# A decoder layer on one core: two heads' value products in one column group, maxima split before they are turned, routing within the cross half

## The chip, the core and the metric

The kernel runs on one core of a Trainium2 chip. The core has a tensor engine (PE, with its weight loads as PEld), VectorE (DVE), ScalarE (ACT), GpSimd (POOL) and SyncE (SP), each with its own queue of instructions; they wait for one another by semaphores. Matmul results stand in PSUM, in 8 banks of 128 partitions x 512 fp32 columns. The metric is the device time of one launch in microseconds.

## The reference

64 sequences of 128 tokens, width 128, 16 heads of 8; a context of 77 tokens per sequence. One decoder layer:

```python
x = x + attn(layernorm(x))                    # q,k,v = h Wq', h Wk', h Wv'; softmax(q k' / sqrt(128)) v, then Wff' + bff
x = x + xattn(layernorm(x), ctx, ctx, mask)   # with bq, bk, bv; softmax(masked q k' / sqrt(8)) v, then Wo' + bo
h = layernorm(x)                              # experts
gate = l2norm(h Wp') . l2norm(sim) / temperature          # 8 experts
top_v, top_i = top_k(gate, 2);  p = softmax(top_v)
x = x + sum over the two of p_e * (gelu(h W1[e] + b1[e]) W2[e] + b2[e])
```

The bias bv of the cross values goes through a softmax whose weights sum to 1, and then through Wo: it adds the constant bv Wo' to every token.

## The kernel before

Stage A holds the attentions, the norms and the routing. It works on blocks of 4 sequences (NS = 4, 16 blocks), in a software pipeline of steps t = -3 to 19, all written out. A step has two halves. In the self half (X, `in_x`) PE makes the exponent scores of self attention of block t and, in between, the scores from which the maxima of block t+1 come; in the cross half (Y, `in_y`) the exponent scores of cross attention of block t-2 and the maxima scores of block t-1. A half has 16 units of 4 heads (half of one sequence's heads of one group g), and 3 more to run out. In each unit u PE does 4 score products for the maxima (`scores`, L982), 4 for the exponent (`shifted`, L998), in every second unit the value products of two units (`values`, L1018), and then what `in_x(u)` or `in_y(u)` hangs on: turnings (transposes), projections, the ranks. Each engine's code has the same steps and the same u, and thus its own fixed order.

Value products: the weight of a head is 32 columns wide (`VW`): 8 values, a column of ones for the denominator, zeros. 4 heads of a unit go to the 4 column groups of PE side by side (partitions 32c to 32c+31 of a bank), and the four units of a sequence fill one bank `pv`. ACT copies each bank to `oT` (L594), PE turns it in four pieces (`outputs_T`, L1048, units 0 to 3 of the next half), DVE divides by the denominator (`divide`, L741, L743). Then the result is turned back (u = 5) and projected (u = 7), DVE adds the residual (u = 8) and takes the norm's statistics.

Maxima: DVE takes them from the score bank (L731). PE turns the negated maxima (`maxima_T`, L961, u = 6), and they are split into three bf16 shares in the turned shape of 16 x 512: ACT (L559), DVE (L719), ACT (L566), POOL (L440). SP writes them to DRAM and reads them back under the stacked queries (`fold`), where they shift the exponent.

Two working banks, `wb[0]` and `wb[1]`, serve all that hangs on: `claim` makes PE wait until the last user of a bank has been read (`drained`).

Norms: DVE statistics, `lnve` (L705), POOL the power -1/2 (L431), DVE `lnnm` (L710), ACT the normalising in four pieces (L572).

Routing of block t-3: the gate's product in Y at u = 10, 11; `choose` on DVE in Y at u = 16 (gate values, the top two, marks, running sums `before`); in X of the next step `weigh` (u = 10), the ranks on PE (u = 15, three products, L1093 to L1097) and `route` (u = 16), which gives each token its two slots. POOL scatters the rows to the experts' lists (`enlist`, 8 indirect DMAs per block, L457), paced by PE's units.

Stage B (`phase_b`) runs over 39 tiles of 512 listed rows and the two expert products; it is not changed. Between the stages DVE builds a table of tiles, and the pipeline has drained.

## Time and profile before

| | us |
|---|---|
| median of 3 runs | 1223.12 |
| lowest, highest | 1222.99, 1224.07 |
| the profiled execution | 1220.65 |
| its span | 1218.9 |
| PE busy in the span | 1027.5 (84%) |
| DVE, ACT, POOL busy | 874.9, 842.9, 552.5 |

The span is what the profile shows between the first and the last instruction. A busy PE is not a PE at its peak, since matmuls are pipelined and their ends are modelled: what a group costs the queue is the distance from its start to the start of the next one, and not its own duration. An engine's idle time before an instruction stands in brackets, with what ended it.

### The profile page before, as it was taken

To read this page: it belongs to the slowest core of one execution; us is meant where nothing else is said; L and a number is where in the kernel's file an instruction comes from. 1 tells how busy PE (TensorE), PEld (TensorE's weight loads), DVE (VectorE), ACT (ScalarE), POOL (GpSimd) and SP (SyncE) were. 2 spreads that over 40 slices of the span, in tenths; PEclk is the share of its full clock that TensorE was granted. 3 is DMA by queue.
4 is the path that set the end of the run, shared out by engine and by line. 5 is a ranking of instruction groups with operands and counts; after the bars stand their busy time and mean duration, and the time that the engine had idled before them with its cause. 6 is when DMAs were issued, how large, how long until landed. Compare 5 with 4: busy or idle time off the path is not lost. (4 is left out here: it accounts for less than half of the span.)

```text
span 1218.9 us, 32475 instructions
## 1 busy us (share of the span) xinstructions
PE 1027.5 (84%) x11795; PEld 792.2 (65%) x11795; DVE 874.9 (72%) x2569; ACT 842.9 (69%) x1729; POOL 552.5 (45%) x550
## 2 busy tenths in 40 slices
PE   2467789999999999999999999967709999999940
PEld 1255567777777777777767777745507888888730
DVE  2655657778788787787887786654367888888846
ACT  1255567778777877777787777644509999998940
POOL 4312323245545544554555444433442666665650
PEclk9877899999999999999999999988858999999985
DMA  4327574473474454545544631430252444232219
GB/s 93 94 74 162 140 162 99 118 180 91 124 173 106 125 150 117 135 130 122 150 110 115 169 92 39 103 78 28 94 191 74 113 118 125 84 79 77 79 43 374
DMA packets 120334, 144.24 MB, mean 118 GB/s; under 512 B 34056, under 2 KB 98472, under 8 KB 115376
## 3 DMA queue, kind: packets, MB, share of 16 engines
q1 hardware_dynamic: 108832, 120.37, 38.8%
q0 software_dynamic: 9168, 17.21, 4.5%
q10 hardware_dynamic: 2176, 4.59, 1.1%
q8 instruction: 95, 1.56, 0.6%
q14 instruction: 63, 0.52, 0.1%
HBM read 88.42 MB, written 55.36 MB: 118 GB/s over the span
## 5 line engine op out<-in xcount | busy, mean ns | idle before, releaser
L584 ACT ACTIVATE probs<-sc_a 77x512 f32<-77x512 f32 (+1 forms) x512 | 300.6, 590 | 122.7 <-PE sc_a L998 51.8
L1295 POOL DMA_INDIRECT y_d<-yo,row x156 | 159.9, 1025 | 117.0 <-issue 81.4
L731 DVE TENSOR_REDUCE negm_m<-sc_m 128x4 f32<-128x512 f32 x256 | 174.1, 684 | 42.9 <-PE sc_m L982 41.1
L731 DVE TENSOR_REDUCE negm_cm<-sc_m 128x4 f32<-128x308 f32 x256 | 119.8, 474 | 108.2 <-PE sc_m L987 102.6
L457 POOL DMA_INDIRECT xs_d<-xrow,slot_i x128 | 127.8, 999 | 141.9 <-PE sc_a L1003 103.9
L1018 PE MATMUL pv<-probs,big 128*32 128x128 f32 x4096 | 165.5, 281 | 0.3
L1390 DVE TENSOR_TENSOR gl<-g,gh 128x512 fp32r<-128x512 f32 x156 | 107.5, 690 | 35.5 <-ACT g L1339 26.7
L1018 PEld LDWEIGHTS pv<-probs,big 128*32 128x32 f32 x4096 | 97.2, 110 | 54.6 <-issue 36.6
L982 PE MATMUL sc_m<-ks,qs 96*128 96x128 bf16 x1024 | 104.6, 229 | 32.2 <-DMA ks<-stk_k 14.0
L982 PEld LDWEIGHTS sc_m<-ks,qs 96*128 96x128 bf16 x1024 | 72.7, 101 | 78.6 <-issue 51.1
L998 PE MATMUL sc_a<-cqs,cks 102*77 102x128 bf16 x1024 | 100.9, 221 | 6.5 <-DMA cqs<-cmscr 6.0
L998 PE MATMUL sc_a<-qs,ks 102*128 102x128 bf16 x1024 | 101.8, 223 | 1.8 <-ACT probs L584 1.8
L1003 PE MATMUL sc_a<-identb,mbias 128*77 128x512 bf16 x256 | 99.2, 387 | 0.0
L998 PEld LDWEIGHTS sc_a<-cqs,cks 102*77 102x77 bf16 x1024 | 89.1, 118 | 14.3 <-issue 6.7
L982 PE MATMUL sc_m<-cks,cqs 96*128 96x77 bf16 x1024 | 79.9, 201 | 20.1 <-DMA cqs<-cmscr 12.7
L982 PEld LDWEIGHTS sc_m<-cks,cqs 96*128 96x128 bf16 x1024 | 63.8, 99 | 41.5 <-issue 23.7
L1048 PE MATMUL wb<-ident,oT 128*128 128x128 f32 x512 | 79.0, 279 | 7.6 <-DVE rest_q L721 5.1
L987 PE MATMUL sc_m<-mbias,identb 128*128 128x308 bf16 x256 | 78.0, 305 | 0.0
L594 ACT ACTIVATE oT<-pv 128x512 f32<-128x512 f32 x128 | 75.9, 593 | 2.4 <-PE pv L1018 1.5
L440 POOL TENSOR_TENSOR parts_m<-rest_k,parts_m 16x512 bf16<-16x512 f32 x32 | 36.7, 1148 | 80.1 <-ACT parts_m L566 80.1
L998 PEld LDWEIGHTS sc_a<-qs,ks 102*128 102x128 bf16 x1024 | 70.1, 99 | 3.9 <-ACT probs L584 2.7
L435 POOL TENSOR_TENSOR xres<-xagain,bff_b 128x512 f32<-128x512 f32 x16 | 20.4, 1274 | 115.2 <-DMA xagain<-x_dram 115.2
(201 smaller groups left out, 2546.7 us busy)
## 6 DMA issues: line engine op xcount, KB each, us to landing
xg<-xs_d SPq DMA_DIRECT2D x39, 260.0 KB
stk_q<-parts_q SPq DMA_DIRECT2D x16, 384.0 KB, 2.5
stk_k<-parts_k SPq DMA_DIRECT2D x16, 384.0 KB
qs<-stk_q SPq DMA_DIRECT2D x16, 384.0 KB
ks<-stk_k SPq DMA_DIRECT2D x32, 192.0 KB
stk_cq<-parts_cq SPq DMA_DIRECT2D x16, 384.0 KB, 2.9
cqs<-stk_cq SPq DMA_DIRECT2D x16, 384.0 KB, 5.4
xin<-x_dram SPq DMA_DIRECT2D x16, 256.0 KB
```

The lines of the kernel that those rows point to most:

```text
L457: nc.gpsimd.indirect_dma_start(out=xs_d, in_=row[:, c // 2, c % 2, :], in_offset=None, out_offset=bass.IndirectOffsetOnAxis(ap=slot_i[:, c ...
L584: nc.scalar.activation(probs[e % 4][0:rows], sc_a[e % 2][0:rows], ACT.Exp, scale=scale)\
L594: nc.scalar.activation(oT[n][:, s, :], pv[s % 2][:], ACT.Copy).then_inc(oT_ok[n].sem, 1)
L731: nc.vector.tensor_reduce(out=negm[n][:, s, g, 4 * half:4 * half + 4], in_=sc_m[u % 2][:, 0:4 * cols].rearrange("p (j k) -> p j k", j=4), ...
L982: i = nc.tensor.matmul(sc_m[u % 2][:, j * cols:(j + 1) * cols], qst[0:KR, 4 * half + j, s * S:(s + 1) * S], kst[0:KR, HG * g + 4 * half + ...
L987: i = nc.tensor.matmul(sc_m[u % 2][:, 0:4 * cols], identb[:], bias[:, s, :].unsqueeze(1).broadcast_to([128, 4, cols]), start=False, stop=T ...
L998: i = nc.tensor.matmul(sc_a[u % 2][0:cols, j * S:(j + 1) * S], kst[:, HG * g + 4 * half + j, s * cols:(s + 1) * cols], qst[:, 4 * half + j ...
L1003: i = nc.tensor.matmul(sc_a[u % 2][0:cols, :], bias[:, s, :], identb[:].unsqueeze(1).broadcast_to([128, 4, S]), start=False, stop=True, sk ...
L1018: i = nc.tensor.matmul(pv[s % 2][32 * c:32 * c + VW, (u % 4) * S:(u % 4 + 1) * S], va[:, s, HG * g + 4 * half + c, :], probs[u % 4][:, c * ...
L1048: i = nc.tensor.transpose(wb[s % 2][:, slot * S:(slot + 1) * S], oT[n][:, s, slot * S:(slot + 1) * S], ident[:])
L1295: nc.gpsimd.indirect_dma_start(out=y12_d, in_=yo[par][:, c, :], in_offset=None, bounds_check=2 * B * S - 1, oob_is_err=False, out_offset=b ...
L1390: nc.vector.tensor_tensor(out=gl[c][:], in0=g[c][:], in1=hi32(gh[c][:]), op=ALU.subtract).then_inc(gl_ok.sem, 1)
```

## The change

1. Two heads, one of each group g, share a column group: their weights are 32 wide as before, but the first has its 8 values and its one in the columns 0 to 8, the second in 16 to 24 (`in_pair`). The second product adds to what the first left (start only at g = 0). Two sequences fill one bank. `oT` has 2 pieces per block (`NO`), so there are 2 copies, 2 groups of turnings and 2 divisions (of 32 x 8 values) per block and half, at u = 0 and 1. The steps behind them move up: turning back at u = 3, projection at 5, residual at 6, statistics at 7. The columns of Wv and the rows of Wff and Wo are put in the new order on the host as they were in the old.
2. Maxima: POOL splits them before they are turned (`shares`, four operations on 64 columns). PE then turns the three shares in one go as four bf16 products with the shares as weights, and one ACT copy of 48 x 512 takes them out.
3. Norms: `lnve` and `lnnm` are POOL's; DVE keeps the statistics.
4. Routing of block t-3 stands in the cross half: gate product at u = 8, 9, `choose` at 12, `mark` at 13, ranks at 15, `weigh` at 15, `route` at 16, with fewer and wider operations; running sums are made by more rank products (3 + 1 to 4 + 4) and not by DVE. The row numbers come from an iota on POOL. The scatters are spread over the whole next step, with two sets of slots.
5. The cross value bias: bv Wo' is added to the output bias once at the start (one product, one addition); ACT copies the cross values where DVE added the bias.
6. The self value product moves from u = 4 to 12 of the cross half, and the turned x2 to bank 1 at u = 14, with cross Q at 16.

The core of the diff (declarations, and the like edits of the second attention, left out):

```diff
-        negm = {n: sa(f"negm_{n}", [128, NS, 2, HG]) for n in ("m", "cm")}
+        negm = {n: sa(f"negm_{n}", [128, NS, H]) for n in ("m", "cm")}
+        left = sa("left", [128, NS, H])
+        third_m = sa("third_m", [128, NS, 3, H], BF16)
...
-        oT = dict.fromkeys("sc", sa("oT", [128, NS, T]))
+        oT = dict.fromkeys("sc", sa("oT", [128, NO, T]))
...
+        def in_pair(tile):
+
+            return tile.rearrange("p q g w -> p q (g w)").rearrange("p q (a b) -> p q a b", b=OW)[:, :, 0:4:3, :]
...
-                    pool.wait_ge(ln_ve[n].sem, ln_ve[n].val(b))
+
+                    pool.wait_ge(ln_st[n].sem, ln_st[n].val(b))
+                    wait_block(pool, ln_ok[n], b - 1)
+                    nc.gpsimd.tensor_scalar(lnve[n][:], lnmv[n][:, :, 1], LN_EPS, None, ALU.add).then_inc(ln_rs[n].sem, 1)
+                    nc.gpsimd.tensor_scalar(lnnm[n][:], lnmv[n][:, :, 0], -1.0, None, ALU.mult).then_inc(ln_rs[n].sem, 1)
+                    pool.wait_ge(ln_rs[n].sem, ln_rs[n].val(b, 2))
                     nc.gpsimd.tensor_tensor(out=lnrs[n][:], in0=lnve[n][:], in1=mhalf[:], op=ALU.pow)\
                         .then_inc(ln_rs[n].sem, 1)
+                    pool.wait_ge(ln_rs[n].sem, ln_rs[n].val(b))
+                    nc.gpsimd.tensor_tensor(out=lnnm[n][:], in0=lnnm[n][:], in1=lnrs[n][:], op=ALU.mult)\
+                        .then_inc(ln_nm[n].sem, 1)
...
+                def shares(n, b):
+
+                    pool.wait_ge(max_ok[n].sem, max_ok[n].val(b))
+                    if n == "cm":
+                        wait_block(pool, filled["m"], b + 2)
+                    else:
+                        wait_block(pool, filled["cm"], b - 3)
+                    nc.gpsimd.tensor_copy(third_m[:, :, 0, :], negm[n][:]).then_inc(split[n].sem, 1)
+                    pool.wait_ge(split[n].sem, split[n].val(b, 1))
+                    nc.gpsimd.tensor_tensor(out=left[:], in0=negm[n][:], in1=third_m[:, :, 0, :], op=ALU.subtract)\
+                        .then_inc(split[n].sem, 1)
+                    pool.wait_ge(split[n].sem, split[n].val(b, 2))
+                    nc.gpsimd.tensor_copy(third_m[:, :, 1, :], left[:]).then_inc(split[n].sem, 1)
+                    pool.wait_ge(split[n].sem, split[n].val(b, 3))
+                    nc.gpsimd.tensor_tensor(out=third_m[:, :, 2, :], in0=left[:], in1=third_m[:, :, 1, :], op=ALU.subtract)\
+                        .then_inc(split[n].sem, 1)
...
+                def enlist(b, c, behind, unit):
+
+                    if c == 0:
                         pool.wait_ge(twin_ok.sem, twin_ok.val(b))
                         pool.wait_ge(slot_ok.sem, slot_ok.val(b))
                         pool.wait_ge(gate_step.sem, gate_step.val(b))
-                    for c in range(lo, hi):
-                        wait_block(pool, st_f["c"], b + 2, 2 * c + 1)
-                        pool.nop(nofuse=True)
-                        nc.gpsimd.indirect_dma_start(out=xs_d, in_=row[:, c // 2, c % 2, :], in_offset=None,
-                                                     out_offset=bass.IndirectOffsetOnAxis(ap=slot_i[:, c:c + 1], axis=0))\
-                            .then_inc(listed.sem, 16)
+                    wait_block(pool, st_f[behind], b + 4 if behind == "s" else b + 2, unit)
...
+                    if on_(t - 2):
+                        shares("cm", t - 2)
...
+                        twin(t - 4, xrow[par])
+                        enlist(t - 4, 0, "s", 2)
...
+                    if on_(t + 1):
+                        shares("m", t + 1)
...
-                            if e % 4 == 3 and e > 4:
-                                out_T(n, b, e // 4 - 1)
+                            if e == 11:
+                                out_T(n, b, 0)
                         between(u)
                     if on_(b):
-                        out_T(n, b, NS - 1)
-
-                def out_T(n, b, s):
-                    act.wait_ge(pv_ok[n].sem, pv_ok[n].val(b, 4 * s + 4))
-                    nc.scalar.activation(oT[n][:, s, :], pv[s % 2][:], ACT.Copy).then_inc(oT_ok[n].sem, 1)
+                        out_T(n, b, 1)
+
+                def out_T(n, b, k):
+                    act.wait_ge(pv_ok[n].sem, pv_ok[n].val(b, 8 * k + 8))
+                    nc.scalar.activation(oT[n][:, k, :], pv[k][:], ACT.Copy).then_inc(oT_ok[n].sem, 1)
...
+                        if u == 5 and on_(t - 1):
+                            if t == 1:
+                                act.wait_ge(preset["cv"].sem, 4)
+                            act.wait_ge(filled["cv"].sem, filled["cv"].val(t - 1))
+                            nc.scalar.activation(in_pair(cvaug[1 - par])[0:SC, :, :, 0:DH],
+                                                 wb[0][0:SC, :].rearrange("p (q g i) -> p q g i", g=NG, i=DH),
+                                                 ACT.Copy).then_inc(drained["cv"].sem, 1)
+                        if u == 7 and on_(t - 2):
+                            evac(parts["cm"][:], "cm", t - 2, 0, rows=3 * H)
...
-                def divide(n, b, s):
-
-                    k = f"oTT_{n}"
-                    dve.wait_ge(filled[k].sem, filled[k].val(b, s + 1))
-                    v = wb[s % 2][:].rearrange("p (h w) -> p h w", w=VW)
-                    nc.vector.reciprocal(rden[n][:, s, :], v[:, :, DH]).then_inc(rden_ok[n].sem, 1)
-                    dve.wait_ge(rden_ok[n].sem, rden_ok[n].val(b, s + 1))
-                    nc.vector.tensor_tensor(out=on[n][:, s], in0=v[:, :, 0:DH],
-                                            in1=rden[n][:, s, :].unsqueeze(2).broadcast_to([128, H, DH]),
-                                            op=ALU.mult).then_inc(drained[k].sem, 1)
+                def divide(n, b, k):
+
+                    key, half = f"oTT_{n}", slice(2 * k, 2 * k + 2)
+                    dve.wait_ge(filled[key].sem, filled[key].val(b, k + 1))
+                    v = wb[k][:].rearrange("p (h w) -> p h w", w=OW)
+                    r = rden[n][:, half].rearrange("p s h -> p (s h)")
+                    nc.vector.reciprocal(r, v[:, :, DH]).then_inc(rden_ok[n].sem, 1)
+                    dve.wait_ge(rden_ok[n].sem, rden_ok[n].val(b, k + 1))
+                    nc.vector.tensor_tensor(out=on[n][:, half].rearrange("p s h i -> p (s h) i"), in0=v[:, :, 0:DH],
+                                            in1=r.unsqueeze(2).broadcast_to([128, 2 * H, DH]),
+                                            op=ALU.mult).then_inc(drained[key].sem, 1)
...
-                    for eq, h in ((eq1, here[0]), (eq2, here[1])):
-                        i = nc.vector.tensor_tensor(out=h[:], in0=eq[:], in1=pos[:], op=ALU.mult)
-                    i.then_inc(gate_step.sem, 1)
-                    dve.wait_ge(gate_step.sem, gate_step.val(b, 15))
-                    for k in range(2):
-                        i = nc.vector.tensor_reduce(out=slot_f[:, :, k], in_=here[k][:], op=ALU.add, axis=AX.X)
-                    i.then_inc(gate_step.sem, 1)
-                    dve.wait_ge(gate_step.sem, gate_step.val(b, 16))
-                    dve.wait_ge(rows_ok.sem, rows_ok.val(b))
-                    nc.vector.tensor_copy(xrow[b % 2][:, :, :, D].bitcast(I32), tok[:])\
+                    nc.vector.tensor_tensor(out=here[:], in0=eq[:], in1=pos[:].unsqueeze(2).broadcast_to([128, NS, 2, E]),
+                                            op=ALU.mult).then_inc(gate_step.sem, 1)
+                    dve.wait_ge(gate_step.sem, gate_step.val(b, 10))
+                    nc.vector.tensor_reduce(out=slot_f[:], in_=here[:].rearrange("p s k e -> p (s k) e"), op=ALU.add, axis=AX.X)\
...
+                        if u == 12 and on_(t - 3):
+                            choose(t - 3)
                         if u == 13 and on_(t - 3):
-                            dve.wait_ge(ss_ok.sem, ss_ok.val(t - 3))
-                            nc.vector.tensor_scalar(ssc[:], ss[:], L2_EPS2, None, ALU.max).then_inc(ssc_ok.sem, 1)
+                            mark(t - 3)
+                        if u == 15 and on_(t - 3):
+                            weigh(t - 3)
                         if u == 16 and on_(t - 3):
-                            choose(t - 3)
...
-                    if u % 4 == 0 and s >= 2:
-                        pe.wait_ge(oT_ok[n].sem, oT_ok[n].val(b, s - 1))
-                    elif u % 4 == 0:
-                        wait_block(pe, oT_ok[last[0]], last[1], s + 3)
+                    if u % 8 == 0:
+                        wait_block(pe, oT_ok[last[0]], last[1], u // 8 + 1)
+                    slot = 2 * (s % 2) + half
                     for c in range(4):
-                        i = nc.tensor.matmul(pv[s % 2][32 * c:32 * c + VW, (u % 4) * S:(u % 4 + 1) * S],
-                                             va[:, s, HG * g + 4 * half + c, :],
-                                             probs[u % 4][:, c * S:(c + 1) * S], start=True, stop=True)
+                        i = nc.tensor.matmul(pv[s // 2][VW * c:VW * (c + 1), slot * S:(slot + 1) * S],
+                                             va[:, HG * s + 4 * half + c, g, :],
+                                             probs[u % 4][:, c * S:(c + 1) * S], start=(g == 0), stop=(g == 1))
...
                 def maxima_T(n, b):
-                    pe.wait_ge(max_ok[n].sem, max_ok[n].val(b))
-                    transposes(n, b, BANK[n], [negm[n][:, s].rearrange("p g j -> p (g j)") for s in range(NS)], H)
-
-                def outputs_T(n, b, s):
-
-                    k = f"oTT_{n}"
-                    claim(s % 2, k, b, s + 1)
-                    pe.wait_ge(oT_ok[n].sem, oT_ok[n].val(b, s + 1))
+                    claim(BANK[n], n, b)
+                    pe.wait_ge(split[n].sem, split[n].val(b))
+                    for s in range(NS):
+                        i = nc.tensor.matmul(wb[BANK[n]][0:3 * H, s * S:(s + 1) * S],
+                                             third_m[:, s].rearrange("p c h -> p (c h)"), identb[:], start=True, stop=True)
+                    i.then_inc(filled[n].sem, 1)
+
+                def outputs_T(n, b, k):
+
+                    key = f"oTT_{n}"
+                    claim(k, key, b, k + 1)
+                    pe.wait_ge(oT_ok[n].sem, oT_ok[n].val(b, k + 1))
                     for slot in range(4):
-                        i = nc.tensor.transpose(wb[s % 2][:, slot * S:(slot + 1) * S],
-                                                oT[n][:, s, slot * S:(slot + 1) * S], ident[:])
-                    i.then_inc(filled[k].sem, 1)
...
+                        if u == 12 and on_(t + 2):
+                            by_token("v", t + 2, 0, xnT["1"], w_v[:], D, S)
...
+                        if u == 15 and on_(t - 3):
+                            claim(0, "rank", t - 3)
+                            pe.wait_ge(gate_step.sem, gate_step.val(t - 3, 5))
+                            rank, total = wb[0][:, 0:NS * E], wb[0][:, NS * E:(NS + 1) * E]
+                            nc.tensor.matmul(rank, tri[:], chosen[:].rearrange("p s e -> p (s e)"),
+                                             start=True, stop=False, skip_group_check=True)
+                            for s in range(1, NS):
+                                nc.tensor.matmul(rank[:, s * E:], ones[:], chosen[:, 0:NS - s, :].rearrange("p s e -> p (s e)"),
+                                                 start=False, stop=(s == NS - 1), skip_group_check=True)
+                            for s in range(NS):
+                                i = nc.tensor.matmul(total, ones[:], chosen[:, s, :], start=(s == 0), stop=(s == NS - 1),
+                                                     skip_group_check=True)
+                            i.then_inc(filled["rank"].sem, 1)
```

Where the order changes. First VectorE at the end of the cross half, in a full step; `negm_cm` are the maxima, `gs` the gate values, `rest_q` the remainder of cross Q. Before:

```order
L731 TENSOR_REDUCE negm_cm<-sc_m 128x4 x2
L762 TENSOR_SCALAR gs<-graw,rn,itemp 128x8 x4
L768 MAX top_v<-gs 128x8 x4
L773 MAX_INDEX top_i<-top_v,gs 128x8 x4
L775 TENSOR_TENSOR dv<-top_v 128x4
L778 CAST top_f<-top_i 128x8
L781 TENSOR_TENSOR eq<-iota,top_f 128x32 x2
L785 TENSOR_TENSOR chosen<-eq 128x32
L788 TENSOR_TENSOR before<-before,chosen 128x8 x4
L721 SCALAR_TENSOR_TENSOR rest_q<-wb,bq_c,parts_cq 128x512
```

And of the changed kernel:

```order
L757 TENSOR_REDUCE negm_cm<-sc_m 128x4 x2
L788 SCALAR_TENSOR_TENSOR gs<-graw,itemp,rn 128x32
L794 MAX top_v<-gs 128x8 x4
L797 TENSOR_TENSOR dv<-top_v 128x4
L800 MAX_INDEX top_i<-top_v,gs 128x8 x4
L757 TENSOR_REDUCE negm_cm<-sc_m 128x4
L806 CAST top_f<-top_i 128x8
L808 TENSOR_TENSOR eq<-iota,top_f 128x64
L813 TENSOR_TENSOR chosen<-eq 128x32
L757 TENSOR_REDUCE negm_cm<-sc_m 128x4 x2
L819 TENSOR_SCALAR den<-ev 128x4
```

The choice has moved from behind the last maximum to between the maxima of units 12, 13 and 14.

Then PE at the start of the self half; `sc_m` and `sc_a` are the scores, `oT` the outputs that are turned. Before:

```order
L982 MATMUL sc_m<-ks,qs 128x128 x4
L1048 MATMUL wb<-ident,oT 128x128 x4
L982 MATMUL sc_m<-ks,qs 128x128 x4
L998 MATMUL sc_a<-qs,ks 128x128 x4
L1048 MATMUL wb<-ident,oT 128x128 x4
L982 MATMUL sc_m<-ks,qs 128x128 x4
L998 MATMUL sc_a<-qs,ks 128x128 x4
L1048 MATMUL wb<-ident,oT 128x128 x4
L982 MATMUL sc_m<-ks,qs 128x128 x4
L998 MATMUL sc_a<-qs,ks 128x128 x4
L1048 MATMUL wb<-ident,oT 128x128 x4
```

And of the changed kernel:

```order
L987 MATMUL sc_m<-ks,qs 128x128 x4
L1056 MATMUL wb<-ident,oT 128x128 x4
L987 MATMUL sc_m<-ks,qs 128x128 x4
L1003 MATMUL sc_a<-qs,ks 128x128 x4
L1056 MATMUL wb<-ident,oT 128x128 x4
L987 MATMUL sc_m<-ks,qs 128x128 x4
L1003 MATMUL sc_a<-qs,ks 128x128 x4
L987 MATMUL sc_m<-ks,qs 128x128 x4
L1003 MATMUL sc_a<-qs,ks 128x128 x4
L966 MATMUL wb<-ident,on 128x128 x4
```

Two of the four groups are gone, and the turning back (`on`) follows two units behind the second.

## Rows read from the trace of the kernel before

**Rows 1.** The page's first part: busy time, share of the span, instructions.
```profile
PE 1027.5 (84%) x11795; PEld 792.2 (65%) x11795; DVE 874.9 (72%) x2569; ACT 842.9 (69%) x1729; POOL 552.5 (45%) x550
```

**Rows 2.** Busy us (instructions) per stretch; then granted clock, DMA share, GB/s.
```profile
145.20:763.60 618.40, 598.58 (x8570) 458.98 (x8567) 483.12 (x1557) 476.10 (x1034) 285.01 (x276) 1.00 0.51 126
763.60:909.30 145.70, 89.78 (x1154) 66.78 (x1151) 75.49 (x341) 65.53 (x161) 62.55 (x65) 0.81 0.33 97
...
430.20:477.80 47.60, 46.59 (x667) 35.83 (x667) 38.53 (x128) 37.31 (x83) 23.94 (x24) 1.00 0.50 130
```

**Rows 3.** In order of time, self half: start, duration, engine, line.
```profile
431.31 0.40 PE L982 MATMUL sc_m<-ks,qs 96*128 96x128 bf16 x4
431.54 0.39 PE L998 MATMUL sc_a<-qs,ks 102*128 102x128 bf16 x4
...
432.39 0.40 PE L982 MATMUL sc_m<-ks,qs 96*128 96x128 bf16 x4
...
430.57 0.68 DVE L731 TENSOR_REDUCE negm_m<-sc_m 128x4 f32<-128x512 f32 x1
431.17 0.25 DVE L741 RECIPROCAL rden_c<-wb 128x16 f32<-128x16 f32 x1
431.45 0.29 DVE L743 TENSOR_TENSOR on<-wb,rden_c 128x128 f32<-128x128 f32 x1
431.66 0.68 DVE L731 TENSOR_REDUCE negm_m<-sc_m 128x4 f32<-128x512 f32 x1
```

**Rows 4.** The same view, PE, cross half.
```profile
453.08 0.60 PE L1048 MATMUL wb<-ident,oT 128*128 128x128 f32 x4
453.51 0.31 PE L982 MATMUL sc_m<-cks,cqs 96*128 96x77 bf16 x4
...
459.62 0.60 PE L961 MATMUL wb<-ident,negm_m 128*16 128x128 f32 x4
460.06 0.31 PE L982 MATMUL sc_m<-cks,cqs 96*128 96x77 bf16 x4
```

**Rows 5.** The same view, PE; in brackets the idle time before.
```profile
447.87 0.39 PE L998 MATMUL sc_a<-qs,ks 102*128 102x128 bf16 x4
448.68 0.19 PE L1093 MATMUL wb<-chosen,tri 128*128 128x32 bf16 x1 [0.42 <-DVE rest_k L719]
448.71 0.18 PE L1095 MATMUL wb<-before,ones 128*128 128x32 bf16 x1
...
476.83 0.65 PE L1048 MATMUL wb<-ident,oT 128*128 128x128 f32 x4 [0.47 <-DVE rest_q L721]
```

**Rows 6.** Groups by line, 145.2 to 763.6 us: busy, mean ns, idle before.
```profile
L594 ACT ACTIVATE oT<-pv 128x512 f32<-128x512 f32 x104 | 61.6, 593 | 0.7
...
L431 POOL TENSOR_TENSOR lnrs<-lnve,mhalf 128x4 f32<-128x4 f32 x36 | 37.7, 1047 | 14.2 <-DVE lnve L705 12.8
L440 POOL TENSOR_TENSOR parts_m<-rest_k,parts_m 16x512 bf16<-16x512 f32 x26 | 29.9, 1149 | 51.2 <-ACT parts_m L566 51.2
L705 DVE TENSOR_SCALAR lnve<-lnmv 128x4 f32<-128x4 f32 x36 | 20.8, 578 | 1.2
...
L480 POOL CAST parts_k<-rest_k 128x512 bf16<-128x512 f32 x12 | 7.3, 608 | 14.2 <-DVE rest_k L719 14.2
```

**Rows 7.** POOL in order of time.
```profile
2.91 0.17 POOL L424 IOTA tok<- 128x8 f32 x1
...
439.05 1.28 POOL L435 TENSOR_TENSOR xres<-xagain,bff_b 128x512 f32<-128x512 f32 x1 [6.31 <-DMA xagain<-x_dram]
```

**Rows 8.** The drain, ACT and POOL in order of time.
```profile
844.72 0.59 ACT L559 ACTIVATE parts_m<-wb 16x512 bf16<-16x512 f32 x1 [0.26 <-PE wb L961]
...
846.76 1.14 POOL L440 TENSOR_TENSOR parts_m<-rest_k,parts_m 16x512 bf16<-16x512 f32 x1 [8.59 <-ACT parts_m L566]
...
880.25 1.06 POOL L457 DMA_INDIRECT xs_d<-xrow,slot_i  x1 [2.10 <-DVE slot_i L827]
...
887.63 1.05 POOL L498 TENSOR_TENSOR rn<-ssc,mhalf 128x4 f32<-128x4 f32 x1
```

360 lines of the change are left out of this document (159 added, 201 removed).

## The prediction

> **What bounds the kernel now.** I read the page's first part, then the busy time by stretches, then the tensor engine's and VectorE's instructions in order of time inside one step, and last the costs by line. The page names the tensor engine first, 84% busy over the whole span [rows 1], but that is an average over three stages. From 145.2 to 763.6 us the pipeline is full: 618.4 us, PE busy for 598.6 of them at the full granted clock [rows 2]. One step there lasts 47.6 us, PE busy for 46.59, DVE for 38.53, ACT for 37.31, POOL for 23.94 [rows 2]; so 618.4 us are 13 full steps. The experts' stage, from 909.3 us to the end of the span, is not touched and keeps its 309.6 us. The 145.7 us between [rows 2] drain the pipeline, and PE is busy for 89.8 of them: there chains of waits decide.
>
> A step is bound by the order of PE's own queue. Two things in the rows say how far. In the cross half the unit row goes on without a hole: four turnings of the outputs start at 453.08 and the next scores at 453.51, so a group of four costs 0.43 us of queue, though its record says 0.60 [rows 4]. In the self half the same group costs more. The scores of one unit start at 431.31 and those of the next at 432.39, 1.08 us apart, while PE's own share is 0.23 + 0.22 + 0.43 = 0.88 us. DVE starts its pieces 0.60, 0.28 and 0.21 us apart, 1.09 in all [rows 3]: with a division beside every maximum, VectorE sets the pace for those four units. Besides, PE waits twice in a step by name: 0.42 us at the ranks, until VectorE has read the K product out of bank 0, and 0.47 us at the second turning of the self half, for VectorE's remainder of the cross Q product [rows 5].
>
> **The change, by its parts, per full step.**
>
> Value products: as many matmuls as before, 4 column groups each, so I cost the products themselves at nothing. That the second product of a pair now adds to what the first left, no row shows; if each of the 16 pairs of a step lost or gained what stands between two small products, 0.03 us [rows 5], it would be 0.5 us either way. What goes is half of what follows: the outputs fill 2 banks per block and half-step, not 4. 8 groups of turnings become 4: 4 x 0.43 = 1.72 us of PE's queue [rows 4], the surest term. ACT loses 4 copies of 0.593 us [rows 6], off the path. DVE divides 4 times where it divided 8 times, each on twice the elements.
>
> Pace in the self half: before, four units with 0.2 us each of waiting for VectorE, 0.8 us. Now two units hold a division; it costs between 0.49 us (as now) and 0.98 us (twice), which with the maximum's 0.60 is 1.1 to 1.6 us against PE's 0.88 [rows 3]. The next two units hold no division, and two score banks let VectorE lag by one unit. I take half of the wait as gone: 0.4 us, ends 0 and 0.8.
>
> Maxima: four fp32 turnings, 459.62 to 460.06, 0.44 us each time [rows 4], become four bf16 products of 128 moving columns; four such score products stand 0.23 us apart in the queue (431.31 to 431.54, [rows 3]). Twice a step: 2 x 0.22 = 0.44 us gained, ends 0 and 0.44. After them comes one ACT copy, where ACT, DVE, ACT and POOL stood one behind the other. The splitting moves ahead of it to POOL, in four short operations on 64 columns. POOL's cast of 512 columns takes 0.608 us and its subtraction 1.149 [rows 6], and one of 8 columns 0.17 [rows 7]: a piece of 64 columns lies between 0.17 and 0.30 us, four with their hand-overs at about 1.3 us. They hide in POOL's wait of 6.31 us for the second load of x [rows 7] in the one half; in the other they are ready some 5 us before PE reaches them. Without that cover they would cost 1.3 us per half-step.
>
> Routing: choosing, ranking and placing stand within one cross half; nothing of it is left in the self half. PE's ranks waited from 447.87 + 0.22 to 448.68, 0.59 us [rows 5]. In the new place the bank is freed by an ACT copy two units earlier, and VectorE has marked its choice about two units ahead: 0.58 us gained, ends 0 and 0.59. Ranks take 8 small products, not 3; two follow each other by 0.03 us [rows 5]: 0.15 us more, ends 0.1 and 0.3. The choice now sits between maxima of the cross half, some 1.6 us of VectorE with unit 13's maximum behind it, for which PE's scores of unit 15 wait. They come over 2 us later, so I take nothing, at most 0.5 us.
>
> Layer norms: POOL takes two small operations before its power and one after it, VectorE loses two of them, one of 0.578 us mean [rows 6]. Per norm POOL's part grows from 1.05 to about 1.9 us, VectorE's shrinks by as much with its queueing. In the cross half ACT's normalising of x2 comes at the tenth unit, about when this chain ends; 0 taken, at most 0.5 us lost. The wait of 0.47 us for the cross Q product [rows 5] stays: its product, ACT copy and remainder keep their order.
>
> The value bias moves into the output bias: an addition on VectorE becomes a copy on ACT, and one product is added at the start, beside the wait for the first stacks. Nothing.
>
> What DVE and ACT lose beyond this (DVE some 8 of its 38.5 us, an estimate from the removed instructions) shortens small waits that are spread over the step: 0.4 us, ends 0 and 1.2.
>
> Sum per full step: 1.72 + 0.4 + 0.44 + 0.58 - 0.15 + 0.4 = 3.4 us, so 44.2 us instead of 47.6; all low ends with the losses together give about nothing, the high ends 4.7; the low ones don't come together, and for the forecast's own range I use 2.1 to 4.5.
>
> **The sum.** 13 full steps x 3.4 = 44.2 us. Five half-filled steps (0, 1, 15, 16, 17) at half of it: 8.5 us, ends 4 and 12. The drain: in step 17 nothing covers the maxima. ACT's first piece starts at 844.72 and POOL's third ends at 846.76 + 1.14 = 847.90 [rows 8], 3.2 us, where one copy of 0.6 stays: 2.6 us. In step 18 the power for the last routing starts at 887.63, behind six row scatters that began at 880.25 [rows 8], 1.26 us apart; now four of them stand after the norm's power and the slots are known earlier: about 2.9 us. Together 5.5 us, ends 2 and 9. Sum 44.2 + 8.5 + 5.5 = 58 us. The profiled execution took 1220.65 us (span 1218.9), so 1162.5; the median of the runs shown is 2.5 us above the profiled execution, which gives 1165.
>
> [...] The lnve addition on VectorE, 4 columns, took 0.578 us in the mean of the full stretch [rows 6], more than three times POOL's 0.17 for 8 columns [rows 7]. The Trainium skill ("SBUF — State Buffer", Who interferes with whom) says that VectorE and GpSimd share a port pair as an exclusive lock, so that one of them can block wholly; the rows agree, and by it each short operation moved to POOL may cost either engine a wait. [...]
>
> **The rivals.**
> - The waits take half back: PE's queue is shorter, but it then stands for ACT and DVE, which are 78% and 81% busy in a step, at the hand-overs (turned outputs to division, maxima's copy to the next use of bank 0, choice to ranks). For it: PE's two named waits are of this kind [rows 5], and bank 0 is handed on to the turned x one unit after ACT's copy. Against it: both engines lose work. Only 1.6 us per full step: 13 x 1.6 + 4 + 4 = 29 us, 1223 - 29 = 1194.
> - VectorE's pace was worth more: all high ends, 4.7 us per step: 13 x 4.7 + 11 + 8 = 80 us, 1143. For it: DVE set the pace of four units [rows 3]; against it: the rest of the self half shows no wait for it.
> - Slower: POOL becomes the bound. Its power on 4 columns costs 1.047 us [rows 6]. If each of the 19 small operations that it gains (8 for maxima, 9 for norms, 2 for routing) costs as much, POOL has 23.9 - 2.3 + 19.9 = 41.5 us of work per step. Its residual of x starts at 439.05, 9 us into the step (which begins at about 430) and for the load [rows 7], and before it only some 6.6 us of work are to be done: 9 + 35 = 44 us, and some 4.5 us of waits in the rest of its order make 48.5, 0.9 us more than now. 13 x 0.9 = 12 us: 1235. It decides from about 0.9 us per small operation. Against it: 0.17 us for the small one [rows 7]; the power is a special case.
> - The change doesn't halve the turnings: excluded, since the order of PE's queue shows two groups where four stood.
>
> **How the numbers follow.** The forecast holds with 0.72 (its own range 1148 to 1183), waits that take half back 0.15, the larger gain 0.08, slower 0.05. The range of 8 in 10 reaches up to the half-back case and down into the larger gain: 1146 to 1194. A measurement of this kernel can tell about 0.2%, 2.4 us, from no change. Faster 0.94, the same 0.01, slower 0.05.
>
> **What would show it.** Right: full steps 43 to 45 us apart, PE at 0.97 or more of them; two turning groups per half-step, no wait at the ranks; DVE near 30 us a step, ACT near 35, POOL 26 to 28; the piece before the experts' stage shorter by about 58 us in all, and that stage at 309 to 310 us. Wrong: PE below 0.95 of a step with waits on ACT or DVE at the turnings, or at the cross norm; POOL's small pieces above 0.5 us; a step of 46 us or more; or value products that stand further apart in PE's queue than before.

## The result and the profile after

The changed kernel takes 1181.54 us (median of 4 runs, 1179.97 to 1185.62) beside 1223.05 us for the kernel before (median of 4, 1221.35 to 1224.07): a ratio of 0.9667, 95% interval 0.964 to 0.9694, 41.5 us less. The forecast was 1165 us: right in direction and inside its range, 16.5 us too low. The profiled execution of the changed kernel is the slowest of its four (1185.62 us), so the two traces differ by only 35.0 us of span.

The page's first part, to be held against [rows 1]: every engine but POOL has less to do, DVE most (125.6 us less).

```profile
span 1183.9 us, 31785 instructions
PE 996.1 (84%) x11621; PEld 767.5 (65%) x11621; DVE 749.3 (63%) x2074; ACT 799.0 (67%) x1649; POOL 593.3 (50%) x821
```

Busy time by stretches of the changed kernel, in the columns of [rows 2]: twelve steps, the drain with the last full step, the experts' stage, then one step and its self half and cross half.

```profile
144.63:686.51 541.88, 523.74 (x7737) 400.81 (x7737) 352.55 (x1094) 404.59 (x894) 291.16 (x450) 1.00 0.55 136
686.51:877.40 190.89, 131.89 (x1832) 98.88 (x1828) 85.60 (x332) 95.57 (x226) 91.97 (x133) 0.84 0.34 95
877.40:1183.90 306.50, 255.89 (x1248) 208.70 (x1248) 240.76 (x484) 248.07 (x430) 160.69 (x156) 0.91 0.39 118
416.31:461.55 45.24, 43.95 (x653) 33.62 (x649) 30.04 (x95) 34.18 (x77) 26.17 (x40) 1.00 0.54 137
416.31:437.80 21.49, 20.23 (x307) 15.37 (x303) 15.64 (x33) 16.85 (x34) 12.44 (x18) 1.00 0.53 132
437.80:461.55 23.75, 23.72 (x351) 18.26 (x347) 14.39 (x62) 17.33 (x43) 13.73 (x23) 1.00 0.55 141
```

The same cuts in the kernel before, without the row of the whole step, made at the same events (the first score product of a half, the first load of the experts' rows):

```profile
144.60:713.04 568.44, 550.65 (x7864) 421.51 (x7862) 445.29 (x1432) 439.54 (x954) 262.95 (x255) 1.00 0.52 130
713.04:910.07 197.03, 138.30 (x1866) 104.85 (x1862) 113.33 (x465) 102.44 (x241) 84.61 (x86) 0.85 0.33 93
910.07:1218.90 308.83, 256.64 (x1248) 208.25 (x1248) 240.60 (x484) 247.56 (x430) 159.86 (x156) 0.91 0.38 117
475.06:497.49 22.43, 21.50 (x318) 16.45 (x314) 20.46 (x56) 18.38 (x37) 10.26 (x10) 1.00 0.55 138
497.49:522.36 24.87, 24.76 (x351) 19.01 (x347) 17.78 (x72) 18.61 (x45) 13.40 (x14) 1.00 0.50 124
```

Of the 35.0 us, 26.5 come in the twelve steps (2.2 each), 6.1 in the drain, 2.3 in the experts' stage, and none in the first 144.6 us. Two things stand out. The cross half is full (PE busy for 23.72 of 23.75 us), the self half is not: 1.26 of its 21.49 us are holes. Here is the head of the self half, PE in order of time, to be held against [rows 3]:

```profile
461.55 0.40 PE L987 MATMUL sc_m<-ks,qs 96*128 96x128 bf16 x4
461.78 0.61 PE L1056 MATMUL wb<-ident,oT 128*128 128x128 f32 x4
...
463.27 0.40 PE L987 MATMUL sc_m<-ks,qs 96*128 96x128 bf16 x4
463.50 0.39 PE L1003 MATMUL sc_a<-qs,ks 102*128 102x128 bf16 x4
464.59 0.40 PE L987 MATMUL sc_m<-ks,qs 96*128 96x128 bf16 x4 [0.69 <-DVE negm_m L757]
...
465.40 0.63 PE L966 MATMUL wb<-ident,on 128*128 128x128 f32 x4 [0.19 <-DVE on L770]
```

and VectorE over the same time:

```profile
461.87 0.75 DVE L747 SCALAR_TENSOR_TENSOR rest_q<-wb,bq_c,parts_cq 128x512 f32<-128x512 f32 x1 [1.63 <-ACT parts_cq L592]
462.53 0.68 DVE L757 TENSOR_REDUCE negm_m<-sc_m 128x4 f32<-128x512 f32 x1
463.13 0.34 DVE L768 RECIPROCAL rden_c<-wb 128x32 f32<-128x32 f32 x1
463.51 0.42 DVE L770 TENSOR_TENSOR on<-wb,rden_c 128x256 f32<-128x256 f32 x1
463.85 0.68 DVE L757 TENSOR_REDUCE negm_m<-sc_m 128x4 f32<-128x512 f32 x1
...
465.17 1.88 DVE L757 TENSOR_REDUCE negm_m<-sc_m 128x4 f32<-128x512 f32 x3
```

VectorE stands idle for 1.63 us, until ScalarE has the first part of cq, and then works without a pause: remainder, maximum, division, maximum, division. A unit with a wide division takes it 1.32 us (462.53 to 463.85), where it took 1.09 with a narrow one [rows 3]. PE's wait of 0.47 us at the second turning [rows 5] is gone; one of 0.69 us, and a start 1.09 instead of 0.23 us behind sc_a, stands two groups later.

The places where the forecast spoke of PE's queue in the cross half, from three spots of it (turning; maxima; ranks):

```profile
438.09 0.60 PE L1056 MATMUL wb<-ident,oT 128*128 128x128 f32 x4
438.52 0.30 PE L987 MATMUL sc_m<-cks,cqs 96*128 96x77 bf16 x4
...
446.46 0.40 PE L1046 MATMUL wb<-identb,third_m 128*48 128x128 bf16 x4
446.79 0.32 PE L987 MATMUL sc_m<-cks,cqs 96*128 96x77 bf16 x4
...
458.52 0.18 PE L1126 MATMUL wb<-chosen,tri 128*128 128x32 bf16 x1
458.73 0.40 PE L1003 MATMUL sc_a<-cqs,cks 102*77 102x128 bf16 x4
```

A turning group 0.43 us, as forecast; the maxima 0.33 us (not 0.23; [rows 4] had 0.44); ranks without a wait, 0.21 us (0.08 before). And the cut of the maxima on POOL:

```profile
440.54 0.23 POOL L443 CAST third_m<-negm_m 128x64 bf16<-128x64 f32 x1
440.86 0.31 POOL L445 TENSOR_TENSOR left<-negm_m,third_m 128x64 f32<-128x64 f32 x1
441.23 0.24 POOL L448 CAST third_m<-left 128x64 bf16<-128x64 f32 x1
441.54 0.31 POOL L450 TENSOR_TENSOR third_m<-left,third_m 128x64 bf16<-128x64 f32 x1
```

1.31 us from 440.54 to 441.85, the forecast's 1.3.

Two more places of PE's queue changed, and the forecast had neither as a term. In the cross half of the kernel before, the scores behind the second turning started 0.71 us behind it, where the others start 0.43 behind; this loss of 0.28 us is gone (439.24 to 439.68 us in the changed kernel). Before:

```profile
498.93 0.60 PE L1048 MATMUL wb<-ident,oT 128*128 128x128 f32 x4
499.64 0.31 PE L982 MATMUL sc_m<-cks,cqs 96*128 96x77 bf16 x4
```

In the self half a wait is new. The normalised x is turned into bank 0, and now waits there for ScalarE's copy of the maxima (`parts_m`). The turning starts 0.88 us behind the value products, where it was 0.58 (486.13 to 486.71 in the kernel before), in each of ten steps. The changed kernel:

```profile
471.82 0.64 PE L1022 MATMUL pv<-probs,big 128*32 128x128 f32 x16
472.70 0.63 PE L966 MATMUL wb<-ident,xn 128*128 128x128 f32 x4 [0.23 <-ACT parts_m L583]
```

### The profile page after: what moved, and what is told of

Read it like the earlier page. It is cut to its first block and busy times, and to the rows that moved or that the text cites. A ratio compares the mean times of both kernels' runs of the same rounds, so it can differ in the third digit from the quotient of the medians.

```text
span 1183.9 us, 31785 instructions
## 1 busy us (share of the span) xinstructions
PE 996.1 (84%) x11621; PEld 767.5 (65%) x11621; DVE 749.3 (63%) x2074; ACT 799.0 (67%) x1649; POOL 593.3 (50%) x821
## 5 line engine op out<-in xcount | busy, mean ns | idle before, releaser
L757 DVE TENSOR_REDUCE negm_m<-sc_m 128x4 f32<-128x512 f32 x256 | 169.5, 683 | 82.5 <-PE sc_m L987 81.4
L477 POOL DMA_INDIRECT xs_d<-xrow,slot_i x128 | 131.9, 1031 | 121.3 <-PE sc_a L1008 80.0
L987 PE MATMUL sc_m<-ks,qs 96*128 96x128 bf16 x1024 | 105.3, 230 | 37.5 <-DMA ks<-stk_k 13.4
L1524 PE MATMUL pv<-gl,vh 128*128 128x512 f32 x156 | 64.7, 415 | 0.0
L1518 PE MATMUL pv<-gh,vh 128*128 128x512 f32 x156 | 62.4, 400 | 0.0
L1519 PE MATMUL pv<-gh,vl 128*128 128x512 f32 x156 | 61.8, 396 | 0.0
```

The lines of the kernel that those rows point to most:

```text
L477: nc.gpsimd.indirect_dma_start(out=xs_d, in_=xrow[b % 2][:, c // 2, c % 2, :], in_offset=None, out_offset=bass.IndirectOffsetOnAxis(ap=slo ...
L757: nc.vector.tensor_reduce(out=negm[n][:, s, HG * g + 4 * half:HG * g + 4 * half + 4], in_=sc_m[u % 2][:, 0:4 * cols].rearrange("p (j k) -> ...
L987: i = nc.tensor.matmul(sc_m[u % 2][:, j * cols:(j + 1) * cols], qst[0:KR, 4 * half + j, s * S:(s + 1) * S], kst[0:KR, HG * g + 4 * half + ...
L1518: nc.tensor.matmul(o, vh[par][:, w], gh[c][:], start=(c == 0), stop=False)
L1519: nc.tensor.matmul(o, vl[par][:, w], gh[c][:], start=False, stop=False)
L1524: nc.tensor.matmul(y_banks[par][:], vh[par][:, c * 128:(c + 1) * 128], gl[c][:], start=False, stop=(c == FC - 1)).then_inc(w2_done.sem, 1)
```

## The experiments

Twelve kernels ran, each beside the kernel before on its chip. The step is the mean of ten (from the first score product at about 190 us on); times of different groups of runs are compared by their ratios, since the kernel before had medians from 1218.8 to 1223.1 us.

| kernel | us | ratio to before (95%) | step, us |
|---|---|---|---|
| before | 1223.1 | 1 | 47.28 |
| the change | 1181.5 | 0.9667 (0.964 to 0.9694) | 45.02 |
| u1 value products unpaired | 1202.3 | 0.9841 (0.9821 to 0.9861) | 46.26 |
| u2 maxima cut behind the turning | 1230.7 | 1.0082 (1.0068 to 1.0096) | 48.14 |
| u3 routing late | 1198.1 | 0.9809 (0.9789 to 0.983) | 46.15 |
| u4 = u2 and u3 | 1220.7 | 1.0 (0.9984 to 1.0015) | 47.60 |
| u5 norms on VectorE | 1189.4 | 0.9745 (0.9722 to 0.9768) | 45.54 |
| u6 = u2, power first | 1200.4 | 0.9838 (0.9814 to 0.9862) | 45.79 |
| u7 value bias on VectorE | 1186.9 | 0.9731 (0.9705 to 0.9756) | 45.07 |
| c1 turnings twice | 1193.0 | 0.9791 (0.9761 to 0.9821) | 45.93 |
| n1 divisions spread | 1178.8 | 0.9653 (0.9639 to 0.9667) | 44.94 |
| n2 cq a unit earlier | 1177.9 | 0.965 (0.9627 to 0.9674) | 44.69 |
| n3 = n1 and n2 | 1174.5 | 0.9625 (0.9601 to 0.9649) | 44.53 |
| n4 = n3, first part of cq ahead | 1171.5 | 0.9603 (0.9581 to 0.9624) | 44.24 |

**u1: the value products unpaired.**

```diff
-    i = nc.tensor.matmul(pv[s // 2][VW * c:VW * (c + 1), slot * S:(slot + 1) * S],
-                         va[:, HG * s + 4 * half + c, g, :], ..., start=(g == 0), stop=(g == 1))
+    i = nc.tensor.matmul(pv[s % 2][VW * c:VW * (c + 1), (u % 4) * S:(u % 4 + 1) * S],
+                         va[:, s, HG * g + 4 * half + c, :], ..., start=True, stop=True)
```

> The changed kernel with the value products as before: a column group of its own for each head of each half, four eviction copies, four turning groups and four narrow divisions in a half instead of two wide ones, at the units at which they stood before; everything else of the change stays. Theory T (the change's gain in a full step is what TensorE's queue lost, 4 turning groups of 0.43 us and a rank wait, and the rest of the forecast's gain was taken back by VectorE, which is late at the head of the self half, where a unit with a wide division costs it 1.32 us): the four groups return, 1.72 us a step, the 0.9 us wait for the first maxima goes, so +0.8 to +1.3 us in each of the 13 full steps and 1 to 4 us at the ends: 1193 to 1203 us against 1181.5. Rival F (the forecast's sum, in which VectorE's head costs nothing and evenly spread work gains beside the groups): +1.7 to +2.1 us a step, 1204 to 1215 us. Both: nothing in the first 144.6 us, which wait for transfers.

Measured 1202.3 us, a step 1.24 us longer: inside theory T's numbers, below the full 1.7 of the forecast. The halves tell more than the sum:

```profile
423.03:444.59 21.56, 20.96 (x315) 16.19 (x311) 16.16 (x37) 17.71 (x36) 11.13 (x17) 1.00 0.51 128
444.59:469.20 24.61, 24.58 (x358) 19.19 (x354) 15.18 (x66) 18.54 (x46) 15.04 (x24) 1.00 0.54 139
```

The cross half is 0.86 us longer, two groups at 0.43. The self half has as many more groups, and is 21.56 us instead of 21.25 (the usual length there; the 21.49 above has one loss of 0.24 us at the turning of the context). PE works 0.9 us more in it and waits 0.5 less. (The experiment also puts the turning back and the projection two units later, as they stood before, so its self half tells of the groups and of that order together.)

**c1: the turnings twice.** It asks for the price of a group directly.

```diff
-    for slot in range(4):
+    for slot in [0, 1, 2, 3] * 2:
         i = nc.tensor.transpose(wb[k][:, slot * S:(slot + 1) * S], oT[n][:, k, ...], ident[:])
```

> The changed kernel with each of the four groups that turn the value products' outputs issued twice into the same bank (the output is unchanged): four more groups of four float32 turnings in a step, with nothing on another engine. It measures the price that the forecast had for the four removed groups, 0.43 us each. If TensorE's queue is the bound where they stand: 1.7 us a step less what the waits at the head take up (0.5 to 0.9 in the self half), so +0.9 to +1.7 us a step, +12 to +24 us in all, 1194 to 1206 us. If the head of the half is bound by VectorE alone: under 0.9 us a step, 1182 to 1192 us.

```profile
372.83:394.08 21.25, 20.79 (x314) 16.25 (x310) 15.54 (x33) 16.75 (x34) 13.52 (x20) 1.00 0.55 134
394.08:418.70 24.62, 24.59 (x359) 19.13 (x355) 14.49 (x62) 17.34 (x43) 12.71 (x21) 1.00 0.53 136
```

Two extra groups cost 0.87 us in the cross half and nothing at all in the self half (21.25 us with and without them): there they only fill what PE waits for VectorE. That is the shortfall of the forecast's surest term in one pair of lines. The whole, 0.91 us a step and 1193.0 us, falls on the border of the two expectations: the queue is the bound in the one half and VectorE in the other.

**u2, u3, u4, u6: the maxima, the routing, and GpSimd's queue.** u2 puts back the turning of the maxima in float32 and the cut behind it; u3 puts the routing back where it stood; u4 does both; u6 is u2 with one line of GpSimd's order moved.

```diff
# u2: PE, ACT, DVE, ACT and POOL in place of POOL, PE, ACT
-    pe.wait_ge(split[n].sem, split[n].val(b)) ... third_m[:, s] x identb
+    transposes(n, b, BANK[n], [negm[n][:, s] for s in range(NS)], H)
+    first("m", t + 1)  # u == 6     remainder("m", t + 1)  # u == 7     second("m", t + 1)  # u == 8
-    shares("m", t + 1)
+    third("m", t + 1)
     enlist(t - 4, 3, "c", 2); enlist(t - 4, 4, "c", 5); power("2", t)
# u3: choose and mark at unit 16, weigh, ranks and route in the next self half
-    enlist(t - 4, 0, "s", 2) ... enlist(t - 4, 1, "s", 6) ... enlist(t - 4, 2, "s", 11)
+    enlist(t - 4, 0, "c", 1); enlist(t - 4, 1, "c", 3); enlist(t - 4, 2, "c", 5)
     shares("m", t + 1)
# u6: u2 with
-    third("m", t + 1); enlist ...; enlist ...; power("2", t)
+    enlist ...; enlist ...; power("2", t); third("m", t + 1)
```

> The changed kernel with the maxima as before: turned in float32 as four turnings of 16 columns, and cut into three parts behind the turning by ScalarE, VectorE and GpSimd. Theory T: only TensorE's queue counts, where the turning took 0.44 us and the four products take 0.33 us: +0.10 us a half, +0.2 us a step, +2.6 us in all, and up to 3 us where steps are half filled and the dump of the maxima is waited for: 1183 to 1188 us. Rival P (the time of the cut on ScalarE and VectorE, 2.3 us a half, delays the two halves' own work): +0.5 us or more a step, 1189 us or more. Rival Q: below 1181 us, if GpSimd's five short operations at the head of its loop cost more than they save.

> The changed kernel with its shorter routing put back where it stood: choice at unit 16 of the cross half, weights at unit 10, ranks at unit 15 and slots at unit 16 of the self half of the next step, scatters in the cross half. Theory T: the wait of the rank products for the remainder of k comes back, 0.42 to 0.58 us a step: +0.4 to +0.6 us a step, 5 to 8 us in full steps, and 2 to 5 us in the drain, which is a part of a step longer: 1188 to 1194 us. Rival F2 (the place is worth nothing, the wait only moves to the next product): 1181 to 1184 us.

> The changed kernel with two parts as before at once: the maxima cut behind their turning, and the routing where it stood; the paired value products, the norms' small operations on GpSimd, the folded bias and the routing's fewer operations stay. Theory Q (in u2 the maxima's cut cost 49 us only because GpSimd's queue holds the norm's power behind the third part of m, and the choice of the same step, now in the cross half, waits for GpSimd in VectorE's queue; so the two parts are one change that works together): with the choice late nothing behind it is urgent, and the price of the whole cut falls to 0 to 6 us over u3's 1198.1: 1196 to 1204 us, below u2's 1230.7 although more is undone. Rival R (the cut itself is the price, by the time that ScalarE and VectorE spend on it): prices add, 1198.1 + 49 = 1240 us or more.

> u2 (the maxima cut behind their turning) with one line moved in GpSimd's queue: the second norm's power, and the two scatters ahead of it, run before the third part of m instead of behind it. Theory Q (u2's 49 us are the power's lateness: in its trace ScalarE waits 3.1 us in each step for lnnm, because GpSimd waits 8.4 us for ScalarE's second part of m and has a third part and two scatters to run before the power): the wait for lnnm falls under 0.7 us, the wait of the choice for rn from 4.7 us to under 1 us, and the kernel takes 1184 to 1195 us. Rival R (the cut costs by its own time on ScalarE and VectorE, wherever GpSimd stands): 1205 us or more.

Theory T fell with u2: not 2 to 6 us but 49, slower than the kernel before. (Rival P's "1189 us or more" is met, but it had no path for so much.) Its trace shows the way. POOL first, in order of time:

```profile
466.00 1.15 POOL L442 TENSOR_TENSOR parts_m<-rest_k,parts_m 16x512 bf16<-16x512 f32 x1 [8.43 <-ACT parts_m L580]
467.31 1.02 POOL L460 DMA_INDIRECT xs_d<-xrow,slot_i  x1 [0.16 <-issue]
...
471.43 0.20 POOL L433 TENSOR_TENSOR lnnm<-lnnm,lnrs 128x4 f32<-128x4 f32 x1
```

then ScalarE:

```profile
471.66 0.49 ACT L586 ACTIVATE xn<-x,lnnm,lnrs 128x128 f32<-128x128 f32 x1 [3.12 <-POOL lnnm L433]
```

POOL waits 8.43 us for a part that ScalarE writes at unit 8, with two scatters and the second norm's power queued behind it; ScalarE waits 3.1 us for the norm in every step, with exponentials behind it, and TensorE runs dry. u6 moves the power and the two scatters ahead, with the same work: 1200.4 instead of 1230.7 us, and the wait for lnnm is gone. So 30 of the 49 us were one place in GpSimd's queue (theory Q's mechanism; its numbers, 1184 to 1195, were too low). What is left, about 20 us, stays with the cut, and 1200.4 us lies between the numbers of theory Q and of rival R (1205 or more). In u6 a self half takes 21.93 us instead of 21.25, with new waits of 0.3 us for rest_k and 0.4 us for a second maximum; steps begin 1.3 us later and the drain is 5 us longer. Which of the cut's four pieces costs this was not taken apart.

u3 is the same kind of case. Ranks without the wait for rest_k were to be its price; that wait did not come back. What its trace shows is a cross half of 24.81 us instead of 23.75, with this

```profile
449.53 0.38 PE L1044 MATMUL wb<-identb,third_m 128*48 128x128 bf16 x4 [1.01 <-POOL third_m L450]
```

once in each step: three scatters, each held to a unit of the cross half, now stand in GpSimd's queue ahead of the cut of m, which TensorE wants at unit 6. The last of the three runs from 447.11 us, the cut from 448.07 to 449.38. 1198.1 us is above theory T's 1188 to 1194, and the trace puts it on the place of the scatters and not on that of the ranks; a u3 with the scatters left where they were did not run. u4 refutes both simple readings: it is 10 us faster than u2 though more is undone (for Q), but 23 us slower than u3 (against Q's 0 to 6); ScalarE's wait of 3.1 us for lnnm is there as in u2, because the power still stands behind the third part. With the maxima and the routing as before, the pairing, the folded bias, the norms and the fewer routing operations together bring nothing in this order: ratio 1.0. The change's parts do not add up one by one. Put back singly they cost, by the ratios, 21 us (u1), 21 (u6), 17 (u3), 10 (u5) and 8 (u7), 77 in all, where the whole change gains 41; so the price of a part put back alone is not its share of the gain.

**u5 and u7: the parts that the forecast had at nothing.**

```diff
# u5
+    nc.vector.tensor_scalar(lnve[n][:], lnmv[n][:, :, 1], LN_EPS, None, ALU.add)   # behind the sums
+    shift("1", t + 2)  # unit 0, self half     shift("3", t - 3)  # unit 13     shift("2", t)  # unit 9
# u7
-    nc.scalar.activation(in_pair(cvaug[1 - par])..., wb[0][0:SC, :]..., ACT.Copy)
+    nc.vector.tensor_tensor(out=in_pair(cvaug[1 - par])..., in0=wb[0][0:SC, :]..., in1=bv_f..., op=ALU.add)
```

> The changed kernel with the norms' small operations on VectorE again: the variance plus epsilon behind the sums, and the shift of the mean one step behind the power, on VectorE at unit 0 (norm 1) and 13 (norm 3) of the self half and unit 9 (norm 2) of the cross half. Theory T: VectorE has two thirds of its time busy, so this costs where it is late, at unit 0 of the self half: 0.15 to 0.3 us there, and a possible stall behind GpSimd's power at unit 9: 2 to 6 us in all, 1183 to 1188 us. The forecast had this part at nothing: 1181 to 1183 us.

> The changed kernel with the bias of the cross values added on VectorE while it copies them (one addition of 77x512 at unit 5 of each self half, as before, 0.68 us), instead of the copy on ScalarE with the bias folded into the output bias; the one-time product for the fold is still issued but not used. Theory T (VectorE is what the self half waits for from its head on, working without a pause until about unit 5, in after's trace): 0.68 us more in that stretch are waited for in part, 0.2 to 0.6 us a step, 3 to 8 us in all, 1185 to 1190 us. The forecast's price, nothing for this part: 1180 to 1183 us.

u5 is slower by 0.0078 in the ratio (about 9 us) and 0.5 us a step, more than either theory had. In every step the shift of 0.15 us stands between VectorE's first maximum and its first division, and the self half is 0.3 us longer. In two of the ten steps it is another 0.9 us longer; in one of them VectorE and then PE stand as follows:

```profile
476.28 1.15 DVE L733 TENSOR_SCALAR lnve<-lnmv 128x4 f32<-128x4 f32 x1
```

```profile
478.08 0.40 PE L995 MATMUL sc_m<-ks,qs 96*128 96x128 bf16 x4 [1.07 <-DVE negm_m L759]
```

and POOL of the same kernel beside it:

```profile
476.14 1.27 POOL L448 TENSOR_TENSOR xres<-xagain,bff_b 128x512 f32<-128x512 f32 x1 [5.99 <-DMA xagain<-x_dram]
```

An addition on 4 columns takes 1.15 us and ends, at 477.43, just behind POOL's residual, at 477.41. This is no accident: of the 32 additions in the eleven steps from 191.48 us on, 25 took 0.17 us, and each of the seven others met a residual or a copy of 512 columns on POOL and ended 0.02 to 0.03 us behind it. POOL's power on 4 columns does not hold it up: ten of the 25 ran beside one. The kernel before shows the same for two of its three additions in each of ten steps, DVE first and POOL behind:

```profile
464.65 0.79 DVE L705 TENSOR_SCALAR lnve<-lnmv 128x4 f32<-128x4 f32 x1
```

```profile
464.26 1.15 POOL L440 TENSOR_TENSOR parts_m<-rest_k,parts_m 16x512 bf16<-16x512 f32 x1 [1.57 <-ACT parts_m L566]
```

VectorE's maxima out of the banks run beside the same POOL operations at their usual 0.68 us. The Trainium skill ("SBUF — State Buffer", Who interferes with whom) says that the two engines hold their shared port pair as an exclusive lock; the trace agrees, with up to 1 us for one small operation. So having the norms' small operations off VectorE is worth 0.5 us a step in this kernel: some 0.3 us by the shift that no longer stands at the head of the self half, and, over the ten steps, some 0.2 us by the lock.

u7 costs next to nothing in a step (45.07 against 45.02), although the 0.68 us fall where VectorE is busy: by the step the forecast's price was right and theory T's 0.2 to 0.6 us wrong. The kernel is 5 to 8 us slower all the same, inside theory T's 1185 to 1190. Between the two profiled executions it is 3.8 us, and 3.2 of them are there before the steps (a self half begins at 194.56 us instead of 191.35). This kernel has one more constant to load at its start, which may be the reason; no run tests it.

**n1 to n4: the head of the self half.**

```diff
# n1: units of the self half
-    outputs_T("c", ...) at 0, 1; divide at 0, 1; divided_T 3; project 5; add_residual 6; stats 7
+    outputs_T("c", ...) at 0, 2; divide at 1, 3; divided_T 5; project 7; add_residual 8; stats 9
# n2: units of the cross half
-    normalise("2") 10-13; x2T 14, its copy 15; product cq 16; first 17; remainder 18
+    normalise("2")  9-12; x2T 13, its copy 14; product cq 15; first 16; remainder 17
# n3: both     n4: both, and
-    first("cq") at 16, behind the last exponential; remainder 17
+    first("cq") at 15, ahead of it; remainder 16
```

> The changed kernel, but in the self half the two turnings of outputs stand at units 0 and 2 and VectorE's two wide divisions at units 1 and 3 instead of 0 and 1, with the turning of the divided outputs, its projection, the residual and the norm's sums each two units later. The work is the same. Theory T (TensorE waits 0.7 to 0.9 us in each self half because the remainder of cq and two wide divisions stand ahead of VectorE's second and third maxima): the wait of sc_m for negm_m shrinks to 0.3 us or less, a full step takes 44.2 to 44.6 us instead of 45.0, and the kernel 1171 to 1177 us. Rival W (VectorE is simply behind by the late remainder and gives the wait back at units 3 and 4): within 2 us of 1181.5, with the wait at a later sc_m.

> The changed kernel with the end of the cross half one unit earlier: the second norm's normalising at units 9 to 12, the turning of x2 at 13, its eviction at 14, the product cq at 15, its first part at 16, its remainder at 17. The work is the same. Theory L (VectorE is behind at the head of the self half because the remainder of cq waits 1.6 us for ScalarE, and ScalarE for the product): the remainder runs before the first maxima are ready, TensorE's wait for negm_m falls from 0.7 us to 0.2 us or less, a step 0.5 to 0.9 us shorter, 1170 to 1176 us. Rival G (the norm's coefficients from GpSimd come too late for it): a new wait of ScalarE for lnnm of over 0.5 us, 1181 us or more.

> n2's earlier cq together with n1's divisions at units 1 and 3. If both levers work on the same lateness of VectorE (theory L), no wait of sc_m for negm_m is left, and the kernel takes 1168 to 1174 us, at most 3 us below n2. If the queue of TensorE alone sets the pace behind the head (rival), n3 is within 1 us of n1's 1178.8.

> n3 with the first part of cq on ScalarE one place further ahead, in front of the last exponential of the cross half instead of behind it (it stood idle there for 1.0 us in n2, waiting for the scores), and the remainder on VectorE at unit 16 behind the slots. Theory L2 (n2 moved the whole end of the half, but the remainder still began 0.26 us behind the first product of the self half, because ScalarE's first part stood behind the last exponential; VectorE is late by that): the remainder ends before the first maxima are there, TensorE's waits for negm_m at units 3 and 4 go or fall under 0.15 us, a step 0.4 to 0.8 us shorter, 1165 to 1170 us. Rival (a unit with a division takes VectorE 1.32 us by itself, so that it is late after two of them from any start): n3's waits stay, 1173 to 1176 us.

n1: rival W is nearer. Two waits of 0.4 us stand where one of 0.7 stood, a step gains 0.1, and the kernel cannot be told from the change. n2's step is shorter, but not as theory L said: the self half keeps its length (21.19 us) and its wait of 0.7 us, because everything moved ahead together and the remainder still begins 0.26 us behind the first product of the self half. Its cross half is 0.3 us shorter, 0.2 of it around the product cq, which no longer stands between the last two groups of value products. n3 is the two added, 1174.5 us; its two waits of 0.4 us stay, so theory L's "no wait left" failed again. n4 moves the remainder itself ahead. VectorE at its head:

```profile
454.43 0.75 DVE L747 SCALAR_TENSOR_TENSOR rest_q<-wb,bq_c,parts_cq 128x512 f32<-128x512 f32 x1 [0.42 <-ACT parts_cq L592]
455.65 1.36 DVE L757 TENSOR_REDUCE negm_m<-sc_m 128x4 f32<-128x512 f32 x2 [0.47 <-PE sc_m L987]
456.93 0.35 DVE L768 RECIPROCAL rden_c<-wb 128x32 f32<-128x32 f32 x1
```

The remainder is done before the first score product (455.22), VectorE now waits for TensorE, and of n3's two waits of PE for maxima one of 0.47 us is left:

```profile
455.22:475.85 20.63, 19.93 (x307) 15.41 (x303) 15.13 (x32) 16.50 (x33) 11.01 (x17) 1.00 0.53 134
475.85:499.44 23.59, 23.57 (x350) 18.31 (x346) 15.25 (x63) 17.55 (x43) 15.23 (x24) 1.00 0.56 144
```

A self half of 20.63 us, against 21.05 in n3, which differs from n4 in this place alone: the late remainder was worth 0.42 us of each self half (the cross half gets 0.13 longer). Against the change it is 0.62 us, the rest being the new units. n4 and n3 can't be told apart by their intervals, only by their steps, 44.24 and 44.53 us. 1171.5 us is a little above theory L2's range, and its rival (n3's waits stay) is half right: a unit with a division still costs VectorE 1.32 us, and one wait stays. n4's interval (0.9581 to 0.9624) lies below the change's (0.964 to 0.9694): n4 beats both kernels. That its step meets the forecast's 44.2 us is a coincidence, since part of it comes from moves in the cross half that the forecast didn't have.

## Why the prediction was right, and what was mis-sized

The time lies inside the range, near the upper end of the forecast's own 1148 to 1183 us. Of its signs, DVE (30.0 us a step), ACT (34.2) and POOL (26.2), the halved turnings and the ranks without a wait came as forecast. A step of 45.0 to 45.2 us is at the edge of "43 to 45", PE's 0.97 is just met, and the part before the experts' stage is 33 us shorter and not 58.

- **The bound.** Right: PE's queue, with VectorE's pace at the head of the self half. The cross half's gain (24.87 to 23.75 us) reads off the queue: two turning groups and the lost 0.28 us 1.15, maxima 0.1, ranks -0.2.
- **Value products, 1.72 us a step.** The price of a group was right (0.43 in c1's cross half), but two of the four stood beside VectorE's work. Undone (u1), the pairing is worth 1.24 us. The missing 0.5 us is the loss of the next point seen from the other side, and is not to be added to it. "At nothing" for the products that add to each other was right: 280 ns each, 281 before, and 16 of them take 0.58 us of the queue in both kernels.
- **Pace in the self half, 0.4 us gained.** This is the step that failed. The forecast priced the wide division right within its ends (1.32 us a unit, with 1.1 to 1.6 given) and then let the two units behind it make it good. It did not put the remainder of cq, which it knew as a wait of 0.47 us "that stays", into VectorE's queue ahead of them. Counted by starts in PE's queue, the head (up to the product of the context's values) lost 1.3 us before: 0.65 at the second turning and the rest beside the divisions. The changed kernel loses 1.46 there: 0.17 and 0.86 at the scores of two units, and 0.43 at the turning back. So 0.15 us is lost where 0.4 was to be gained, 0.55 us a step. n4, held against n3, shows that the place of the remainder alone is worth 0.42 us of a self half; n4 in all gives 8 us by the ratios and 10 by the medians.
- **Maxima, 0.44 us.** 0.2 us by the queue (a group takes 0.33 us, and had been sized by score products that stand 0.23 apart). And the turning back of the maxima has a price that the forecast had only for the drain: the cut undone costs 20 us in the better of the two orders tried (u6) and 49 in the other (u2), by waits on ACT, DVE and POOL.
- **Routing, 0.58 less 0.15.** The wait of 0.59 went, the ranks took 0.13 more. Its place matters for another reason than the one given: scatters in GpSimd's queue (u3).
- **Norms, bias, at nothing.** Bias right by the step (u7). Norms wrong by about 0.5 us a step (u5): the forecast saw the 0.578 us of the addition and named the lock, but counted it as a risk for the operations that moved to POOL, not as a cost of those that stayed on VectorE.
- **Relief from fewer operations, 0.4 us.** Not seen in the self half, where DVE's 15.5 instead of 20.5 us shortened no wait. The 0.28 us of the cross half may be this; no run tells. Against it stands a wait that the forecast had only in a rival, at the hand-over of bank 0 from the maxima's copy to the turned x: 0.30 us a self half.
- **Edges.** The start was to give 3.4 us (two half-filled steps) and gave none: in the first 144.6 us PE is busy for 84.5, and its longest waits are for the stacked keys (13.4 us) and the maxima under the queries (10.1) by DMA and for ScalarE's first normalising (12.9). Drain, last full step and three half-filled steps were to give 14 us and gave 6.1. The experts' stage, forecast unchanged, gave 2.3.

Per step by the queue: turnings 1.72, head -0.15, maxima 0.22, ranks 0.46, the loss in the cross half 0.28, the hand-over of bank 0 -0.30. That is 2.2 us, and the steps measure 2.26, against 3.4 forecast; the pace is half of what is missing. In all: twelve steps 40.8 forecast and 26.5 measured, start 3.4 and 0, drain 14 and 6.1, experts 0 and 2.3: 58 against 35.0 us between the two profiled executions. By the medians the gain is 41.5 us, so the miss is 16.5; about 7 us of it are the mis-sized pace, and the drain's 8 us weigh as much. The rival "waits take half back" named the right mechanism and two of the places, the output's division and the hand-over of bank 0; it took a third of a step's gain, not half. GpSimd as the bound was refuted: 26.2 us a step, in the forecast's 26 to 28.

Two readings of the forecast were off without harm. The self half of the step that it read begins at 427.49 us and not at about 430, so the residual at 439.05 us stands 11.6 us into it and not 9. And its 47.6 us is one of the longer steps; ten of them average 47.28.

Open: the drain, where the forecast's 14 us were not followed up; and the 2.3 us of the experts' stage. It took 308.8 us in the one trace of the kernel before and 306.3 to 307.5 in all thirteen others, so no single part that an experiment put back brings it. Also open is whether the kernel before with the power first would keep part of the gain, which was not run.

## What to carry to other kernels

A group of instructions that leaves the queue of the bounding engine is worth its time only where that engine does not wait soon after; doubling the group and reading the result half by half shows it in one run. When a wait is said to stay, follow what queues behind the waiting instruction on its engine in the new order as well. And an operation on a lightly loaded engine that works in order, such as GpSimd here, can have its price by its place and not by its work: one that waits 8 us for an input, put ahead of a norm's power, cost 30 us. Last, parts put back one at a time need not add up to the whole.

## What the runs showed of the hardware

GpSimd's operations on 4 to 64 columns took 0.20 to 0.31 us each (4 columns 0.20 to 0.24, 64 columns 0.24 for a cast and 0.31 for two inputs), while its power on 4 columns took 1.05. VectorE's reciprocal rose from 0.25 us for 16 columns to 0.35 for 32, and its product out of the bank from 0.29 us for 128 columns to 0.42 for 256: twice the elements, 1.4 times the time. A VectorE operation on 4 columns in SBUF waited for the whole of a 512-column operation on POOL that it met (0.17 us alone, up to 1.15 beside one). Pairs of value products that add into one group ran as fast as single ones (280 and 281 ns each).
